# The last block's scatters spaced over five expert tiles ahead of held-back stores, nine result buffers, and three token tiles summed by ScalarE and GpSimd

## The reference

```
probs = softmax(x @ Wr); topk_w, topk_idx = top_k(probs, 2); topk_w /= sum(topk_w)
for i in range(8):
    w_i = sum(topk_w * (topk_idx == i))
    h = silu(x @ Wg[i]) * (x @ Wu[i])
    output += w_i * (h @ Wd[i])
return x + output
```

## Time and profile before

| | |
|---|---|
| median of 3 runs | 671.04 us (670.31 to 672.01) |
| the profiled execution | 671.66 us, span 669.8 us |
| TensorE matmul busy | 599.4 us, 89% |
| VectorE, ScalarE, GpSimd busy | 74%, 50%, 37% |
| chain that ended last | TensorE 67%, VectorE 16%, ScalarE 9%, issue 5% |
| GpSimd's stores | 39, 37.6 us |
| GpSimd's scatters | 32, 32.8 us |
| expert stage | about 542 us to 654 us |

### The profile page before, as it was taken

One profiled execution on the slowest core, in us unless ns is written; L12 is line 12 of the kernel. 1 busy time (PEld: TensorE's weight loads), 2 busy tenths in 40 slices (PEclk: granted clock), 3 DMA queues, 4 the chain that ended last, 5 costly groups with the idle time before them and its releaser, 6 DMA issues.

```text
span 669.8 us, 14896 instructions
## 1 busy us (share of the span) xinstructions
PE 599.4 (89%) x5522; PEld 454.1 (68%) x5522; DVE 494.1 (74%) x1173; ACT 336.5 (50%) x1175; POOL 251.2 (37%) x228
## 2 busy tenths in 40 slices
PE   2787989998899999999999999999987889799990
PEld 1556777777778766776777766777655578688880
DVE  4899799998366797737987389874885876555567
ACT  1377999999572024741157212670336844355550
POOL 2104000000003853833457834766445513643432
PEclk9897999998799999999999999999997999799996
DMA  8699990000000000000000120002036113333376
GB/s 288 174 337 342 325 319 8 2 2 1 1 2 17 17 0 3 2 1 17 1 2 2 64 64 1 2 9 94 12 107 210 49 48 95 113 110 110 98 258 212
DMA packets 40583, 58.96 MB, mean 88 GB/s; under 512 B 14944, under 2 KB 35040, under 8 KB 39872
## 3 DMA queue, kind: packets, MB, share of 16 engines
q1 hardware_dynamic: 34096, 45.94, 22.3%
q0 software_dynamic: 3408, 9.34, 3.8%
q10 hardware_dynamic: 3008, 2.72, 1.3%
HBM read 46.56 MB, written 29.40 MB: 113 GB/s over the span
## 4 chain that ended last, share of the span: by engine, by line
PE 67%; DVE 16%; ACT 9%; issue 5%; DMA 1%; another core or an unknown queue 1%; ACTq 0%; DVEq 0%
PE bank L395 58%; PE bank L404 9%; ACT ex L1675 2%; DVE x L1574 2%; ACT kbd L1665 2%; DVE nmax L1082 1%; DMA lncol<-in_L_attn_ln_kv_b 1%; DVE wlo L1507 1%; DVE m L1181 1%; ACT ex L1785 1%; DVE yr L1044 1%; DVE hvar L1049 1%; DVE newton L1065 1%; ACT xth L1631 1%
## 5 line engine op out<-in xcount | busy, mean ns | idle before, releaser
L1946 POOL TENSOR_TENSOR r<-m,m 128x512 f32<-128x512 f32 x80 | 104.4, 1328 | 102.1 <-DVE m L1181 87.7
L1181 DVE TENSOR_TENSOR m<-bank,cst 128x512 f32<-128x512 f32 x192 | 121.8, 683 | 24.5 <-PE bank L395 20.1
L1785 ACT ACTIVATE ex<-bank,nmax 128x64 f32<-128x64 f32 x256 | 73.1, 337 | 24.3 <-DVE nmax L1473 24.3
L395 PE MATMUL bank<-xth,wbh 128*128 128x512 f32 x192 | 79.9, 416 | 0.0
L395 PE MATMUL bank<-xth,wbl 128*128 128x512 f32 x192 | 75.2, 392 | 0.0
L395 PE MATMUL bank<-xtl,wbh 128*128 128x512 f32 x192 | 75.0, 390 | 0.0
L1768 ACT ACTIVATE qc<-bank 128x512 f32<-128x512 f32 x32 | 17.4, 595 | 101.8 <-PE bank L395 101.8
L395 PE MATMUL bank<-wop,qc 128*128 128x256 f32 x256 | 62.1, 388 | 0.0
L1993 POOL DMA_INDIRECT results<-ys,place x39 | 37.6, 965 | 62.2 <-ACT ys L1857 57.9
L395 PEld LDWEIGHTS bank<-wop,qc 128*128 128x128 f32 x256 | 46.4, 190 | 13.6 <-issue 7.2
L1675 ACT ACTIVATE ex<-bank,nmax 128x64 f32<-128x64 f32 x256 | 54.3, 357 | 2.5 <-DVE nmax L1082 2.4
(11 more groups left out here) (241 smaller groups left out, 1426.9 us busy)
## 6 DMA issues: line engine op xcount, KB each, us to landing
slots<-in_fill SPq DMA_DIRECT2D x1, 17544.0 KB, 65.3
xs<-slots SPq DMA_DIRECT2D x39, 129.0 KB
gb<-results SPq DMA_DIRECT2D x6, 512.0 KB, 4.7
wo_s<-in_L_xattn_Wo SPq DMA_DIRECT2D x1, 2048.0 KB, 18.1
wq_s<-in_L_xattn_Wq SPq DMA_DIRECT2D x1, 2048.0 KB, 11.8
wraw<-in_L_ffn_Wg SPq DMA_DIRECT2D x8, 256.0 KB, 3.8
wraw<-in_L_ffn_Wu SPq DMA_DIRECT2D x8, 256.0 KB, 4.1
wraw<-in_L_ffn_Wd SPq DMA_DIRECT2D x8, 256.0 KB, 4.8
```

Source lines behind the costliest of these rows:

```text
L395: return e.matmul(o, l, r, start=start, stop=stop, skip_group_check=True)
L1181: last = e.tensor_tensor(m4[n % 2][m][:, :].rearrange("p (b s) -> p b s", s=S), products[half][:, :].rearrange("p (b s) -> p b s", s=S), t ...
L1785: last = e.activation(ex[b % 4][:, h * 64:(h + 1) * 64], score_banks(b)[odd][:, n * 64:(n + 1) * 64], ACT.Exp, bias=nmax[b % 4][:, 4 * odd ...
L1946: last = e.tensor_tensor(rope[n % 6][half][:, :], m4[n % 2][first][:, :], m4[n % 2][second][:, :], op)
```

## The change

1. On GpSimd, stores 0 to 4 stand first, then the eight scatters of the last block, then stores 5 to 38. The scatters and stores 5 to 20 each wait for a signal of the step: in turn the low part of a tile (t_xl), a down product (t_down) and a gate/up product (t_proj), three in two steps (`after_part`). The scatters begin with step 8 as base, the stores with 13.
2. Nine `ys` buffers instead of six. The three new ones lie where the softmax's copies `ssb` were.
3. Token tiles 9 and 11 are scaled and added as tile 12 was, ScalarE ahead of its DMA of tiles 4 to 7. That DMA and the next wait for fewer adds of VectorE, the next for GpSimd's adds of 9 and 11 too.
4. Two semaphores of the biases are replaced by higher counts of a third (not shown).

```diff
-YS = 6
+YS = 9
+        ssb_at = keep.at
         ssb = [keep(f"ssb{i}", [P, 512]) for i in range(2)]
-        ys = [s7(f"ys{i}", [P, D]) for i in range(YS)]
+        over_ssb = Space(nc, ssb_at)
+        ys = [s7(f"ys{i}", [P, D]) for i in range(6)] + [over_ssb(f"ys{i}", [P, D]) for i in range(6, YS)]
...
-            return t - int(t > SUMMED_APART)
+            return t - sum(q < t for q in SUMMED_APART)
...
-        LAST_SCATTERS = {6: (0, 1), 7: (2, 3), 8: (4, 5), 9: (6, 7)}
+        SCATTERS_FROM = 5
+        SCATTER_STEP, STORE_STEP = 8, 13
+        STORES_PACED = 16
-        SUMMED_APART = 4 * EARLY
+        SUMMED_APART = (9, 11, 4 * EARLY)
...
             for t in range(tiles + 2 - COMBINE_FROM, NT):
-                if t != SUMMED_APART:
+                if t not in SUMMED_APART:
...
-            w.wait_ge(t_comb, 16)
+            def scaled(t):
+                n, m = GB_OF[t]
+                for k in range(2):
+                    w.wait_ge(r_shares, 2)
+                    w.wait_ge(d_gb[n], 16)
+                    part = gb[n][:, m, k, :]
+                    e.activation(part, part, ACT.Copy, scale=share[:, t, k:k + 1]).then_inc(t_scaled, 1)
+
+            for t in SUMMED_APART[:2]:
+                scaled(t)
+            w.wait_ge(t_comb, 2 * combined(8))
             e.dma_start(ov[:, 4:8, :], x3[:, 4:8, :]).then_inc(d_out, 16)
...
-            w.wait_ge(t_comb, 24)
+            scaled(SUMMED_APART[2])
+            w.wait_ge(t_comb, 2 * combined(12))
+            w.wait_ge(t_summed, 4)
             e.dma_start(ov[:, 8:12, :], x3[:, 8:12, :]).then_inc(d_out, 16)
...
-            for i in range(sum(TILES)):
-                for n in LAST_SCATTERS.get(i, ()):
-                    w.wait_ge(t_hT, i + 2)
-                    scatter(3, n)
+            def after_part(step, n):
+
+                if n % 3 == 0:
+                    w.wait_ge(t_xl, step + 2 * (n // 3) + 2)
+                elif n % 3 == 1:
+                    w.wait_ge(t_down, step + 2 * (n // 3) - 1)
+                else:
+                    w.wait_ge(t_proj, step + 2 * (n // 3) + 2)
+
+            for i in range(SCATTERS_FROM):
                 store(i)
-            t = SUMMED_APART
-            for k in range(2):
-                w.wait_ge(t_scaled, k + 1)
-                w.wait_ge(t_summed, k)
-                e.tensor_tensor(tile(t), tile(t), gb[GB_OF[t][0]][:, 0, k, :], ALU.add).then_inc(t_summed, 1)
+            for n in range(8):
+                after_part(SCATTER_STEP, n)
+                scatter(3, n)
+            for i in range(SCATTERS_FROM, sum(TILES)):
+                if i < SCATTERS_FROM + STORES_PACED:
+                    after_part(STORE_STEP, i - SCATTERS_FROM)
+                store(i)
+            for n, t in enumerate(SUMMED_APART):
+                at, m = GB_OF[t]
+                for k in range(2):
+                    w.wait_ge(t_scaled, 2 * n + k + 1)
+                    w.wait_ge(t_summed, 2 * n + k)
+                    e.tensor_tensor(tile(t), tile(t), gb[at][:, m, k, :], ALU.add).then_inc(t_summed, 1)
...
-            w.wait_ge(t_summed, 2)
-            result(SUMMED_APART, SUMMED_APART + 1)
+            w.wait_ge(t_summed, 6)
+            result(SUMMED_APART[2], SUMMED_APART[2] + 1)
```

More of the change, by code:

```diff
@@ L334, in decoder @@
         s_w1h, s_crh = sem("w1_high"), sem("crow_high")
-        s_cvps, s_cvT, s_obps, s_borow = sem("value_bias_T"), sem("cvT_made"), sem("out_bias"), sem("borow_made")
+        s_cvT, s_borow = sem("cvT_made"), sem("borow_made")
         s_stat, s_mv, s_var, s_top, s_rstd, s_xhat = (
@@ L632, in values_bias_T @@
                 w.wait_ge(s_crow, 1)
-                transposes(e, [(bank[6][:, k * P:(k + 1) * P], crow[:, 2 * D + k * P:2 * D + (k + 1) * P]) for k in range(KD)]).then_inc(s_cvps, 1)
+                transposes(e, [(bank[6][:, k * P:(k + 1) * P], crow[:, 2 * D + k * P:2 * D + (k + 1) * P]) for k in range(KD)]).then_inc(s_bias, 1)
             def output_bias():
@@ L639, in output_bias @@
                     last = mm(e, bank[7][:, 0:D], cvT[:, k, :], wo1[:, k, :], k == 0, k == KD - 1)
-                last.then_inc(s_obps, 1)
+                last.then_inc(s_bias, 1)
             def keys_T(n):
@@ L1139, in out_bias @@
             def out_bias():
-                w.wait_ge(s_obps, 1)
+                w.wait_ge(s_bias, 3)
                 e.tensor_tensor(borow[:, :], bank[7][:, 0:D], brow[:, 3 * D:4 * D], ALU.add).then_inc(s_borow, 1)
@@ L1690, in values_bias @@
             def values_bias():
-                w.wait_ge(s_cvps, 1)
+                w.wait_ge(s_bias, 2)
                 e.activation(cvT[:, :, :], bank[6][:, 0:2 * P].rearrange("p (k c) -> p k c", k=KD), ACT.Copy).then_inc(s_cvT, 1)
@@ L1876, in scalar @@
                     e.activation(behind[:, :], behind[:, :], ACT.Tanh, scale=0.5).then_inc(r_tanh, 1)
-            w.wait_ge(t_comb, 16)
-            e.dma_start(ov[:, 4:8, :], x3[:, 4:8, :]).then_inc(d_out, 16)
-            t = SUMMED_APART
-            for k in range(2):
[L1881 to L1884, removed]
-            w.wait_ge(t_comb, 24)
+            def scaled(t):
[8 more added lines that the diff above has]
+            w.wait_ge(t_comb, 2 * combined(8))
+            e.dma_start(ov[:, 4:8, :], x3[:, 4:8, :]).then_inc(d_out, 16)
+            scaled(SUMMED_APART[2])
+            w.wait_ge(t_comb, 2 * combined(12))
+            w.wait_ge(t_summed, 4)
             e.dma_start(ov[:, 8:12, :], x3[:, 8:12, :]).then_inc(d_out, 16)
@@ L1996, in gpsimd @@
             route_step(3, -1, ROUTE_LAST)
-            for i in range(sum(TILES)):
-                for n in LAST_SCATTERS.get(i, ()):
-                    w.wait_ge(t_hT, i + 2)
-                    scatter(3, n)
-                store(i)
-            t = SUMMED_APART
-            for k in range(2):
-                w.wait_ge(t_scaled, k + 1)
-                w.wait_ge(t_summed, k)
-                e.tensor_tensor(tile(t), tile(t), gb[GB_OF[t][0]][:, 0, k, :], ALU.add).then_inc(t_summed, 1)
+            def after_part(step, n):
[6 more added lines that the diff above has]
+            for i in range(SCATTERS_FROM):
+                store(i)
+            for n in range(8):
[11 more added lines that the diff above has]
+                    e.tensor_tensor(tile(t), tile(t), gb[at][:, m, k, :], ALU.add).then_inc(t_summed, 1)
             e.drain().then_inc(s_phase, 1)
```

## The result

The changed kernel takes 665.11 us (median of 20 runs, 663.41 to 668.47), the kernel before beside it 671.00 (20 runs): ratio 0.992 (0.991 to 0.993), so 0.8% faster, clear of the noise. The forecast was 664.3 in 663.0 to 669.5; it is 0.8 us too low. The profiled execution took 666.33 us, span 664.2, where 665.0 was forecast for one of its kind.

| | before | after |
|---|---|---|
| gate/up of tile 0 starts | 541.62 | 541.51 |
| from there to gate/up of tile 38 (the stage) | 107.1 | 102.0 |
| from there to the end (the tail) | 21.0 | 20.7 |

What follows compares the result with a forecast made beforehand. It took TensorE to bound the expert stage, stopped once for 6.98 us by late signals. The terms -6.98 + 0.3 + 0.2 - 0.2 = -6.7 against 671.04 gave 664.3 us, range 663.0 to 669.5.

Steps and rivals of the forecast that it cites:

- The stall and its cause: Expert stage, tiles 11 to 13: TensorE loses 6.98 us as its signals arrive late while GpSimd issues DMAs without pause.
- half cured: Rival, chance 0.2: at 1.3 to 1.7 us a DMA signals still come late, 2 to 5 us back, 666 to 669.
- Term 1: GpSimd's new order in the expert stage: stall and lost clock go, -6.98 us, with +0.3 left over the scatter stretch.
- signs named: The two: tile 12's gate/up 2.54 us behind tile 11's; no "remote" before a silu or a ys copy.
- three scatters in a row: Attention part: after three scatters a context product was copied at once, so three in a row cost nothing.
- The start times: GpSimd's eight scatters: 568.76, 570.0, 571.3, 572.7, 574.1, 575.7, 577.8, 579.1; held stores from 580.4.
- Term 2: Held stores in the expert stage: with nine ys buffers no copy waits for a store, 4.5 us to spare, 0.
- Term 3: SP's load of tile 17, 3.7 us behind the last scatter, 0.9 us of slack: +0.2, bounds 0 and +1.
- Term 4: The end hangs on GpSimd's 6.64 us drain, not VectorE's four fewer adds: -0.2; 1.4 of 2.1 us go back.
- the rate is not the cause: Rival, chance 0.1: scatters as such or loads beside them cause the stall, which moves and keeps its size, 669.5 to 672.
- The slower one: Rival, chance 0.1: paced stores make signals late by 1.1 us a step, deciding from 7 of 14 steps, 675 to 679.

Runs made afterwards that it cites:

- stores_close_again: Changed kernel, stores from 5 on without spacing, scatters still spaced, where the kernel before takes 670.76 us: 672.56 us, ratio 1.002.
- stores_close: Changed kernel, stores from 5 on without spacing, scatters still spaced, where the kernel before takes 663.22 us: 661.41 us, ratio 0.998.
- pause_and_two: Changed kernel with three scatters back to back, a pause of 2.8 us, then five, and token tile 12 back on VectorE: 664.22 us, ratio 0.991.
- after_again: The changed kernel, unchanged, run once more where the kernel before takes 670.76 us: 664.69 us, ratio 0.991.
- order_alone: Changed kernel with token tiles 9 and 11 back on VectorE, where the kernel before takes 663.22 us: 662.69 us, ratio 0.998.
- before_again: The kernel before, unchanged, run once more for its profile: 671.03 us, ratio 1.000.
- no_apart: Changed kernel with all 16 token tiles summed on VectorE, none apart: 665.09 us, ratio 0.991.

## Why the prediction was right, and where not

**The stall and its cause**: right. TensorE was stopped by its own late signals, and they are late where GpSimd issues back to back; stores_close_again shows that by putting the train elsewhere. What the prediction did not say, since no profile of one chip shows it, is that this holds for some chips only. On the others, variants of the changed kernel with nine buffers gained 0.2 to 0.4% instead of 0.8 to 0.9%. And the rate is not all: the attention part's late signal that spoke for half cured, with single scatters and pairs around it, is in every late trace, after the change too (518.13, idle 3.56 us, "remote").

**Term 1, -6.98 + 0.3**: the -6.98 is right, the residue was mis-sized: it is 1.05 us at tile 12, and 0.77 more at tile 17's step, and two of the signs named were not seen: tile 12 comes 3.59 us behind tile 11, not 2.54, and a silu still waits for "remote". I took it near the row of three scatters in a row, and counted three ahead of the signal at 572.37. Three do stand ahead of it (it is 572.28 now), but the fourth follows at 572.45 without a pause. My start times put the fourth 0.77 us behind its signal; a scatter starts 0.28 us behind (scatter 6 of stores_close at 573.00, the low half done at 572.72, after 1.12 us of waiting), so its wait for VectorE's 571.83 held nothing back. pause_and_two confirms the reading of three: with a real pause after them the loss is 0.2 us, close to the 0.3.

**The start times**: 568.66, 569.92, 571.19, 572.45 against my 568.76, 570.0, 571.3, 572.7; then 574.72, 575.98, 578.57 and 579.86, each 0.3 to 0.8 us later than I said, as the waits are for steps that are themselves 1.05 us late. The held stores came at 581.13 for 580.4.

**Term 2, nine buffers, 0**: right. No copy waits for a store after; with six one does, for 2.60 us, at the copy that I named, tile 11's.

**Term 3, the load of tile 17, +0.2**: the 3.7 us held in the profile of after (579.86 to 583.51), and so did the landing (583.38 to 585.53 in after_again, 2.15 us for my 2.3). But in after_again the load comes 5.6 us behind the last scatter (577.82 to 583.38), and TensorE waits for it. It costs 0 in after, 1.2 in after_again, past the upper bound of 1, and 0.6 in order_alone, where I took 0.2.

**Term 4, the end, -0.2**: right in size, 0.3 in this pair of profiles (21.0 to 20.7; 0.6 in before_again and after_again), and in mechanism: the drain, 6.64 us, behind the adds of tile 12. The contention was under-estimated. VectorE's adds of the whole tail, before and after:

```profile
L1574 DVE SCALAR_TENSOR_TENSOR x<-gb,share,x 128x256 f32<-128x256 f32 x30 | 15.1, 504 | 1.4
```

```profile
L1578 DVE SCALAR_TENSOR_TENSOR x<-gb,share,x 128x256 f32<-128x256 f32 x26 | 15.0, 576 | 1.2
```

Four adds fewer, and 0.1 us less work. I had let 1.4 of 2.1 us go back; nearly all did. At the 483 ns that an add takes in no_apart, where nothing stands beside it, 26 are 12.6 us; of the 2.4 over that, 0.6 was there before beside tile 12's adds (0.83 and 0.76 for 0.49), and 1.8 came with the four new ones, 0.46 each. The chain of waits shows them beside GpSimd's four (651.11 to 654.44):

```profile
650.28 0.50 DVE x L1578
...
650.87 1.27 DVE x L1578
...
652.17 0.84 DVE x L1578
```

The Trainium skill (SBUF — State Buffer, on the shared port pair) has the two engines exclude each other for a whole instruction; by that rule the estimate was 3.3 us, four times 0.82. The trace agrees only in part: the 0.46 us that each add cost is between my 0.35 and the rule's 0.82, and the first one, 0.78 over its usual 0.49, looks like the rule. So four adds moved to GpSimd took 0.1 us of work off VectorE.

**Rivals.** Half cured (0.2) had the mechanism of what was left: one signal late at the old place, one past it, and in after_again a late tile 17; its price of 2 to 5 us was too high, as 1.8 came of it. That the rate is not the cause is refuted on late chips by stores_close_again; scatters back to back, with no store among them, were never run on one. The slower one, that the paced stores spread the trouble, had one case in fourteen steps (the silu of tile 15, 1.5 us late, stores 1.27 and 1.43 us apart), where it needed seven; it did not come. Without the pacing of the stores there was a slower kernel, 672.56 us, but by a train and not by paced stores.

**Against the medians**: in the profiled pair -5.1 in the stage, -0.3 in the tail, -0.1 ahead of them make -5.5 us; the medians say -5.9.

## What to carry to other kernels

Look at what ends the idle time of a consumer: where its producer had long finished and the row says "remote", the signal was late, and the engine to look at is whichever issued work without a pause at that time, here GpSimd with indirect DMAs 1.27 us apart. Pauses behind every second to fourth brought 5 of 7 us back here; a signal that fell in a pause behind three DMAs was on time, and four in a row cost TensorE 0.7 to 1.2 us. Before you say how late a signal is, follow the program's order to find whose it is. Time such a change on several chips before you count on it: a profile of one can show a stall of 7 us that the next one doesn't have. And cost work moved to GpSimd with what it does to VectorE beside it.

## What the runs showed of the hardware that was not expected

- Late signals go with the chip that a run fell on: where the kernel before took 670.8 to 671.5 us they are there, where it took 662.7 to 663.2 they are not. In the seven traces from prompt chips no wait ends by "remote", in spite of trains of 12 DMAs; each of the seven from late ones, before and after among them, has the same pair on VectorE in the attention part. What differs between the chips, and whether a chip keeps to its state, stays open.
- On a late chip, a signal due within 0.2 us of the start of the fourth DMA of a row was 1.3 to 2.1 us late (572.28 to 574.36 in after, 581.93 to 583.84 in pause_and_two, 570.49 to 571.82 in after_again), and in longer trains the lateness grows: 5.4 us for the copy of tile 8 and 6.7 for the silu of tile 11 in the kernel before (product done at 574.93, silu at 581.62), 7.85 in stores_close_again. One that fell in a pause behind three was on time, one that fell on the third of three stores was 1.5 us late.
- GpSimd's last drain lasts 6.64 us whether it begins at 651.9, 653.8, 655.1 or 657.1, behind its adds, and 7.18 us in no_apart, right behind the last store.
